# Four layers over eight items: the next item's opening at the end of the search's stream, setup in two parts, a new weaving table

## What is computed

```python
x = L0_attn_x                                   # 8 x 512 x 128
xn = _layernorm(x, axis=-1)
s = _L0_attn_ref(xn, Wq, Wk, Wv, Wbeta, Wg, Wout, ln_g, ln_b)   # 16 heads of 8: recurrence over tokens
g = _silu(_L0_ffn_ref(xn, ...))                 # a small network, three cycles
x = x + s * g
...
s = _L1_attn_ref(xn, ...)                       # two time-mixing layers
g = _silu(_L1_ffn_ref(xn, ...))                 # two layers of attention in windows of 64, and an ffn
...
s = _L2_attn_ref(xn, ...)                       # state space: 256 channels x 16 states
g = _silu(_L2_ffn_ref(xn, ...))                 # 4 experts, 2 per token
...
s = _L3_attn_ref(xn, ...)                       # 16 heads of 8: softmax kept to each row's 25 largest, and a linear part
g = _silu(_L3_ffn_ref(xn, ...))
```

```python
q = _l2norm((x @ Wq).reshape(b, s, nh, d))
k = _l2norm((x @ Wk).reshape(b, s, nh, d))
beta = jax.nn.sigmoid(x @ Wbeta)
out = out * jax.nn.silu(x @ Wg)
```

## Time and profile before

| | us |
|---|---|
| three runs: median (lowest to highest) | 5226.68 (5222.0 to 5237.3) |
| the profiled execution's own time | 5220.98 |
| its span, first to last instruction | 5219.2 |
| PE, DVE busy | 3965.6, 3970.4 |
| ACT, POOL busy | 2966.9, 2533.0 |
| PE's mean granted clock | 0.822 |

### The profile page before, as it was taken

One profiled execution on the slowest core, in us unless ns is written; L12 is line 12 of the kernel. 1 busy time (PEld: TensorE's weight loads), 2 busy tenths in 40 slices (PEclk: granted clock), 3 DMA queues, 4 the chain that ended last, 5 costly groups with the idle time before them and its releaser, 6 DMA issues. The chain is left out here.

```text
span 5219.2 us, 58396 instructions
## 1 busy us (share of the span) xinstructions
PE 3965.6 (76%) x16712; PEld 1848.2 (35%) x16712; DVE 3970.4 (76%) x7862; ACT 2966.9 (57%) x5742; POOL 2533.0 (49%) x2332
## 2 busy tenths in 40 slices
PE   5777788868878678777788677886887777877676
PEld 2332244423443234432344224442344323443233
DVE  3335678967889678886888868896788967888698
ACT  3443556645666456655666466664566645665443
POOL 1214255453555445562555625545455545556365
PEclk9876889968998789977899688996899878997555
DMA  1000000000000000000000000000000000000000
GB/s 81 1 25 0 5 1 1 25 3 3 1 25 1 3 3 1 25 1 3 3 1 25 1 5 1 8 18 3 3 1 25 1 3 3 1 25 1 2 1 3
DMA packets 7995, 44.07 MB, mean 8 GB/s; under 512 B 848, under 2 KB 848, under 8 KB 7248
## 3 DMA queue, kind: packets, MB, share of 16 engines
q1 hardware_dynamic: 7632, 39.89, 2.0%
HBM read 37.52 MB, written 2.36 MB: 8 GB/s over the span
## 5 line engine op out<-in xcount | busy, mean ns | idle before, releaser
L2054 DVE MAX8 m<-top 128x8 f32<-128x512 f32 x2048 | 1290.7, 679 | 6.4 <-ACT top L1988 5.9
L2117 POOL TENSOR_SCALAR top<-top,m 128x512 f32<-128x512 f32 x512 | 809.9, 1582 | 836.6 <-DVE m L2054 670.2
L2058 DVE MATCH_REPLACE8 top<-m,top 128x512 f32<-128x512 f32 x1536 | 1026.3, 675 | 0.2
L290 PE MATMUL bank<-arena,consts 128*128 128x512 f32 (+1 forms) x912 | 627.7, 782 | 90.7 <-POOL arena L1662 45.4
L2123 POOL TENSOR_TENSOR top<-top 128x512 f32<-128x512 f32 x512 | 654.6, 1278 | 37.5 <-ACT top L1996 20.2
L290 PE MATMUL bank<-arena,weights 128*128 128x512 f32 (+5 forms) x992 | 553.9, 678 | 65.8 <-DVE arena L1242 29.0
L1927 PE MATMUL bank<-consts,top 128*128 128x128 f32 x2048 | 389.5, 322 | 210.6 <-POOL top L2123 128.7
L290 PE MATMUL bank<-arena 128*64 128x128 f32 (+3 forms) x3200 | 464.3, 366 | 54.4 <-ACT arena L1105 53.8
L2003 ACT ACTIVATE top<-bank 128x512 f32<-128x512 f32 x512 | 305.5, 597 | 296.4 <-PE bank L1927 294.8
L1927 PEld LDWEIGHTS bank<-consts,top 128*128 128x128 f32 x2048 | 283.2, 165 | 489.8 <-POOL top L2123 274.8
L290 PE MATMUL bank<-top,vt 128*9 128x128 f32 x4096 | 340.7, 321 | 151.8 <-ACT top L2003 128.2
(11 more groups left out here) (297 smaller groups left out, 6436.9 us busy)
## 6 DMA issues: line engine op xcount, KB each, us to landing
arena<-experts_dram SPq DMA_DIRECT2D x32, 768.0 KB, 6.6
weights<-weights_dram SPq DMA_DIRECT2D x1, 6982.0 KB, 19.2
hold<-x_dram SPq DMA_DIRECT2D x9, 256.0 KB, 2.8
out_dram<-x_out SPq DMA_DIRECT2D x9, 256.0 KB, 3.5
consts<-consts_dram SPq DMA_DIRECT2D x1, 1759.5 KB, 23.6
rot<-consts_dram SPq DMA_DIRECT2D x1, 1024.0 KB, 25.6
```

The costliest lines, as they stand in the source:

```text
L290: return nc.tensor.matmul(o, lhsT, rhs, start=start, stop=stop)
L2054: nc.vector.max(m8[:, slot(p, e), k], src).then_inc(SB["top"], 1)
L2058: nc.vector.match_replace(wk_[e], m8[:, slot(p, e), k], sc[slot(p, e)] if k == 0 else wk_[e], -3e38).then_inc(SB["rest"], 1)
L2117: nc.gpsimd.tensor_scalar(pp[e], sc[slot(p, e)], m8[:, slot(p, e), TOPK // 8, 0:1], None, ALU.is_ge).then_inc(SB["kept"], 1)
```

## The change

1. The opening goes to the end of stream b, eight steps behind the search, for the item of the *next* block. It uses the search's banks (`O`) and tiles of `top`, waits for the `x0` load and for the search's last readers, and DVE's `xn0` waits for layer 2's `du`. Layer 0 starts with V. A new block between setup and `run(0, ...)` computes item 0's opening; item 1's stands at the end of item 0's block, where stream b idles for as many steps as a search has. The loop's last pass computes an opening that nobody reads.
2. Layer 2's gate tile moves out of `hold` (`spare[3]` is the next item's `sg`) and its last product goes to `L.xr`.
3. Setup waits for three loads: the first 1,938 columns of the weights, `x0` and the constants. The rest of the weights and `rot` are waited for in layer 0 of item 0, from its 13th step (`also`), where the moved arithmetic stands (`late_pe`, `late_act`, `late_dve`).
4. `SEARCH` has new digits. Stream a is now 192 steps without the opening (200 before), b 258 (250).

```diff
-SEARCH = ("0100001101010110313101111102014430103203524241042002012030121030211001100413012310002320321101061200"
+SEARCH = ("0211001223120111101111012062132022120226313101020020023111203i02730013205201221133211120011101101110"
...
-                    sp.dma_start(w_sb[:], w_in).then_inc(S["loaded"], 16)
+                    sp.dma_start(w_sb[:, 0:cut], w_in[:, 0:cut]).then_inc(S["loaded"], 16)
                     sp.dma_start(x0, x_in[0]).then_inc(S["loaded"], 16)
                     sp.dma_start(c_sb[:], c_in[:, 0:once]).then_inc(S["loaded"], 16)
-                    sp.dma_start(rot[:].rearrange("p n t -> p (n t)"), c_in[:, once:]).then_inc(S["loaded"], 16)
+                    sp.dma_start(w_sb[:, cut:], w_in[:, cut:]).then_inc(SL["rest"], 16)
+                    sp.dma_start(rot[:].rearrange("p n t -> p (n t)"), c_in[:, once:]).then_inc(SL["rest"], 16)
...
-                    v.wait_ge(S.sem["loaded"], 64)
+                    v.wait_ge(S.sem["loaded"], 48)
...
+        O = [X[1], Y, P, X[0]]
...
-                self.sq, self.rs, self.ksq, self.qsq, self.rk, self.rq, self.beta = (carve() for _ in range(7))
+                self.sq, self.rs, self.ksq, self.qsq, self.rk, self.rq, self.beta = *sc, *ex, wk_[0]
...
-            def pe(self, pe):
+            def pe(self, pe, item, search):
                 S = self.S
-                mm(A[0], C("centre"), x0).then_inc(S["op_xc"], 1)
+                if item:
+                    pe.wait_ge(SD.sem["x0"], 16)
+                if search:
+                    pe.wait_ge(*SB("sc", 2 * NP))
+                    pe.wait_ge(*SB("of", 1))
+                    pe.wait_ge(*SB("took", NT))
+                mm(O[0], C("centre"), x0).then_inc(S["op_xc"], 1)
...
-                mm(self.last, W("l0_Wg"), xn0).then_inc(S["op_g"], 1)
+                if search:
+                    pe.wait_ge(*SB("m", 1))
+                mm(O[3], W("l0_Wg"), xn0).then_inc(S["op_g"], 1)
...
+                if item:
+                    v.wait_ge(*S2("du", 1))
                 v.wait_ge(*S("op_rs", 1))
-                tt(xn0, A[0], self.rs, ALU.mult).then_inc(S["op_xn"], 1)
+                tt(xn0, O[0], self.rs, ALU.mult).then_inc(S["op_xn"], 1)
...
-            yield from L.op.pe(pe)
             cp = L.cp.pe(pe)
-            pe.wait_ge(*S("op_kn", 1))
-            pe.wait_ge(*S("op_qn", 1))
             mm(A[1], W("l0_Wv"), xn0).then_inc(S["v"], 1)
...
+        def b_pe(pe, item, search):
+            if search:
+                cp = Layer3.cp.pe(pe)
+                yield from l3_pe(pe, cp)
+            else:
+                yield from idle("search " * SEARCH_STEPS)
+            if item:
+                yield from (opening if search else lead).pe(pe, item, search)
...
+        def also(steps, more):
+
+            for n, kind in enumerate(steps):
+                if n >= 12:
+                    next(more, None)
+                yield kind
+            for _ in more:
+                pass
...
-            yield from l0_pe(pe)
+            yield from also(l0_pe(pe), late_pe(pe)) if first else l0_pe(pe)
...
+        with nc.Block(no_gpsimd_drain=True) as block:
+            @block.tensor
+            def _(pe):
+                weave(lead.pe(pe, False, False), None)
...
+        lead_marks.settle()
+        clear(top_marks.sems.values())
         run(0, True, False)
```

More of the change, by code:

```diff
@@ L715, in build @@
             POOL=f"nmx {2 * NP},kept {2 * NP},pp {2 * NP}")
+        opening = Opening(top_marks.layer(**OPENING))
+        lead_marks = Marks(nc, ctx, "b")
+        lead_marks.sems = top_marks.sems
+        lead = Opening(lead_marks.layer(**OPENING))
         class Layer0:
@@ L830, in l0_pool @@
             S, L = S0, Layer0
-            yield from idle("hop hop hop hop hop hop hop hop")
             cp = L.cp.pool(g)
-            g.wait_ge(*S("op_sg", 1))
             nc.gpsimd.tensor_scalar(L.sgb, sg, W("l0_ln_b"), None, ALU.mult).then_inc(S["shifted"], 1)
@@ L1350, in __init__ @@
                 L.nm = L.carve(NT)
-                L.sq, L.rs, L.left, L.gate = spare[0:4]
+                L.sq, L.rs, L.left = spare[0:3]
+                L.gate = L.carve()
                 L.xg = [spare[4], L.xr]
@@ new lines, in b_act, with b_dve @@
+        def b_act(a, item, search):
+            if search:
+                cp = Layer3.cp.act(a)
+                yield from l3_act(a, cp)
+            else:
+                yield from idle("search " * SEARCH_STEPS)
+            if item:
+                yield from (opening if search else lead).act(a)
+        def b_dve(v, item, search):
+            if search:
+                cp = Layer3.cp.dve(v)
+                yield from l3_dve(v, cp)
+            else:
+                yield from idle("search " * SEARCH_STEPS)
+            if item:
+                yield from (opening if search else lead).dve(v, item)
@@ new lines, in b_pool, with late_pe @@
+        def b_pool(g, item, search):
+            if search:
+                cp = Layer3.cp.pool(g)
+                yield from l3_pool(g, cp)
+            else:
+                yield from idle("search " * SEARCH_STEPS)
+            if item:
+                yield from idle("hop " * 8)
+        def late_pe(pe):
+            S = SL
+            pe.wait_ge(S.sem["rest"], 32)
+            for n, (name, part) in enumerate((name, part) for name in ("gamma", "beta") for part in range(2)):
+                r = nc.tensor.transpose(X[0][:, 128 * n:128 * n + 128], W(f"l3_{name}", lo=128 * part, n=128), C("ident"))
+            r.then_inc(S["by_channel"], 1)
+            for i in range(DEPTH):
+                for n, name in enumerate(("Wk", "Wv", "Wr")):
+                    mm(X[1][:, DEPTH * n + i:DEPTH * n + i + 1], W(f"l1_{name}{i}"), W(f"l1_ln_b{i}"))
+                for n, (o, w) in enumerate(HCH):
+                    at = 8 + 6 * i + 2 * n
+                    mm(X[1][0:w, at:at + 1], W(f"l1_w1_{i}", lo=o, n=w), W(f"l1_lb{i}"))
+                    r = mm(X[1][0:w, at + 1:at + 2], W(f"l1_w1_{i}", lo=HID + o, n=w), W(f"l1_lb{i}"))
+            r.then_inc(S["shifts"], 1)
+            yield
@@ L2177, in a_dve @@
         def a_dve(v, first):
-            yield from l0_dve(v, first)
+            yield from also(l0_dve(v, first), late_dve(v)) if first else l0_dve(v, first)
             yield from l1_dve(v)
```

183 lines of the change are left out of this document (89 added, 94 removed).

## The result

| | before | after |
|---|---|---|
| median (lowest to highest), us | 5224.93 (5222.0 to 5237.3) | 5134.86 (5130.29 to 5150.64) |
| the profiled execution's own time | 5220.98 | 5130.29 |
| its span | 5219.2 | 5128.5 |
| PE's mean granted clock | 0.822 | 0.822 |

A forecast was written before the change was run, and what follows sets the result against it. Bound by neither one engine nor one chain: two streams whose in-order queues hold each other up, with a bare block start. Setup -25.7 + 8, item 0's tail +10, loop -39.2: total -46.9, 5174 us; range 5105 to 5240.

The forecast's parts named there:

- Part 1, the start: Start of each block: the opening leaves it and V comes first, gaining 16.6 us, net 13.6 a block.
- The norm of the search: Block start: the search's norm now stands between layer 0's matmuls; cost 3 us a block, between 0 and 6.7.
- Part 2, the end: State loop's end: the opening placed there costs 8 us in a middle block and 10 in item 0.
- the ring: Item 0's state loop: 4.07 us round a state, PE in it at the low clock, so added matmuls are paid.
- The rival's 5114: State loop's end and block start: opening hides better, tail 3.3 and norm 0 in place of 8 and 3; chance 0.18.
- The full stall: State loop: the opening's chain overlaps nothing, 18.0 and two table loads, 20.6 us a block; 5273, slower; chance 0.10.
- Part 3, setup: Setup in two parts: loads land 17.3 us earlier, arithmetic shrinks by 11.4, new boundary costs 3; net -25.7.
- the new boundary: Behind the first opening, with 12 clears per engine: taken as 3 us, between 0 and 8.
- The late work: Item 0's layer 0: setup arithmetic moved there, 40 matmuls of 8.2 us and a sigmoid; costs 8, between 0 and 10.8.
- Part 4, the table: Search steps redistributed across the block: counted as 0, with -5 and +10 us a block as ends.
- the rival's size: Layer 1's first attention: the item stands 24.5 us, thinned places return little over half; +10 a block, 5244; chance 0.12.
- the burst: Layer 1's first attention: 18 search steps in one gap, 24.5 us in which the item stands.

The follow-up runs named there:

- experiment 1: Changed kernel with the old table up to the state loop and the new table inside it: 5128.14 us, ratio 0.9800 against the kernel before.
- experiment 2: Kernel before with the new table alone, behind eight zeros for the opening's steps: 5302.05 us, ratio 1.0143.
- experiments 4 and 5: Changed kernel, loop's opening replaced by cheap stand-ins: 5146.27 us; the same with eight unread matmuls put back at its places on PE: 5136.68 us.
- experiment 6: Kernel before with the matmul that spreads B issued twice in each of the 16 states: 5230.19 us, ratio 1.0004.
- Experiment 3: Changed kernel with all eight steps of the opening behind the layer's last instruction, at the block's very end: 5289.34 us, ratio 1.0115 against the kernel before.
- experiments 9 and 10: Changed kernel with a bigger burst, 34 search steps in one gap: 5241.31 us; with the old table ahead of the states and 22 steps in one gap: 5292.66.
- experiment 7: Changed kernel with setup waiting for all five loads again: 5146.49 us (two runs), ratio 0.9839 against the kernel before.

## Why the prediction was right, and where its sizes were off

The direction, the range (5105 to 5240) and most mechanisms held. The forecast's gain of 47 stands against 90.7 by the two spans: 30 of the missing 44 us are in the loop, 11 in item 0, 2 in the last search. That the total fell well inside the range is partly luck. The forecast added up the moved opening and the new table as if one did not change the other's price, and counted the table at nothing. Measured one behind the other in the profiled blocks, with the table first, the table costs 10.3 a block and the opening then gains 20.5; with the opening first it gains 6.8 and the table another 3.4. Either way the sum is 10.2, where the forecast had 5.6.

- **Part 1, the start.** 16.6 forecast, 17.1 measured. The norm of the search was counted at 3, and no cost of it shows (in experiment 1 the start fell by 17.8, V's share was 16.8): the lower of the two ends that the prediction kept.
- **Part 2, the end: the term that was mis-sized most.** "At the low clock PE is in the ring, so a matmul put there is paid" was worked out from item 0's ring, and gave 8 a block and 10 in item 0. Measured is 5.2 beside the old table (experiment 1), and -2.3 beside the new one (217.3 to 215.0, experiment 2 against the change). In item 0, from the experts' loads to the store, it is 188.5 in place of 189.3. Two things in the ring's sum were wrong. It left the clock where it was: the added matmuls came with a granted 0.73 in place of 0.50 (experiments 4 and 5; the kernel before, with the old table, had 0.61 to 0.66 there), and in item 0 with 0.83 between 480 and 500, where the stretch that lies as far ahead of the store before, 499 to 519, had 0.50:

```profile
480.00:500.00 20.00, 14.11 (x27) 5.06 (x28) 13.61 (x14) 12.37 (x19) 16.14 (x10) 0.83 0.00 0
```

  And it read the ring as closed: experiment 6 put up to 10 us of PE work in it for 0.4 to 1.9 a block, and for 2.8 in item 0. The prediction had this as a rival ("high clock in the tail, because it adds PE work, and a free norm") and set against it that item 0 was at 0.50; but that was the clock without the work that the change puts in. The rival's 5114 overshoots by 16 against the profiled execution: 13.3 a block in place of 9.9, with the table at nothing.
- **The full stall** is refuted for this place. Experiment 3 gives the size that the rival had without its table loads, 18.0 a block, for an opening laid behind the states. The price of a table load is 1.28 us as before. In item 0's opening after the change, ACT:

```profile
25.57 1.28 ACT L311 ACT_TABLE_LOAD   x1
26.86 0.69 ACT L606 ACTIVATE top<-bank,consts 128x512 f32<-128x512 f32 x1
```

  The next ACTIVATE starts 0.01 us behind the load. The Trainium skill (ScalarE: Activation LUTs, What ACT_TABLE_LOAD costs) states a drain of 1.38 us besides; this trace again shows none, and the price would have moved the sum away from the result.
- **Part 3, setup.** -25.7 forecast and -25.8 measured at V (landing 10.43 against 10.5 forecast; the new boundary, from `u`'s end at 30.66 to V at 32.83, 2.2 against 3). The late work was counted at 8. From V to the experts' load item 0 took 289.65 in place of 282.01: 7.6 more, 2.0 of it up to the `x0` load and 5.6 behind it. In the other runs with the same late work it was 287.6 to 290.9, of which 64 to 71 us up to the `x0` load. So the term's size was right, but not its reason: the 40 matmuls took 0.60 + 3.79 = 4.4 us in place of the 8.2 of the earlier trace rows, in a stretch at the high clock (1.00 from 68 to 74). Where the rest of the 7.6 lies was not taken apart.
- **Part 4, the table.** 0 forecast, with -5 and +10. As a part of the change it is about neutral (experiment 1). But it isn't so alone: in the kernel before it costs 10.3 a block (experiment 2), the rival's size for another reason. The forecast weighed only the burst. What the table takes from the block's start is given back nearly one for one (9.2 for 9.4), what it takes from the end is not (12.2 for 19.1), unless the opening stands there: in the change the end is 14.5 shorter than before for 16.6. A cost of the burst itself does not show (the middle grew by 31.6 with 31.2 to 31.5 of DVE work); experiments 9 and 10 show what makes a burst cost, steps taken from the gaps behind it.
- **The sum by what was measured**: first store -19.0 in place of -7.7 (-25.8 at V, +7.6 to the experts' load, -0.8 from there; forecast -25.7, +8 and +10); loop -69.4 in place of -39.2; last search -2.3 in place of 0.

One block of the seven is 8 us longer than the others (615.5, the middle 304.8). Within its second attention 0.50 was granted, with PE busy 16.9 of 20 us:

```profile
3879.70:3899.70 20.00, 16.89 (x82) 9.30 (x82) 10.34 (x28) 10.29 (x36) 8.50 (x11) 0.50 0.00 0
```

In the middle block the stretch as far behind the store (3272 to 3292) had 0.74. Two of seven blocks had a middle of 304 to 305 in experiment 2, none in experiment 7. What triggers one was not tried and stays open.

## What to carry to other kernels

A dependent chain of small operations that stands bare at a boundary is worth its length when it is laid between the steps of another loop, and costs that length again when it is laid bare elsewhere (18.0 us behind the states; between them 5.2 beside the old table and less than nothing beside the new one). Two edits that use the same room have no price of their own each: run each alone and both together before the terms are added up. Sum the busy time of the fullest engine by stage, before and after: where a stage's length and that work change alike (31.6 and 31.5), the work was only moved, and the gain is in the stage whose idle time fell. When filler work is concentrated, look at the gaps that it is taken from: a full engine cost nothing here, but the serial stretch behind it must keep its cover.

## What the runs showed of the hardware

Matmuls added to a stretch in which PE was granted half clock cost less than their durations at that clock: eight of 128x512 made the end 1.8 us shorter (217.3 to 215.5), with the grant 28 to 13 us ahead of the store going from 0.50 in all seven blocks to 0.70 to 0.73, and the output matmul behind them taking 1.99 us in place of 3.78. Sixteen of up to 0.63 us, spread over all states of the kernel before, cost 0.4 to 1.9 a block, and 2.8 in item 0. A busy PE was not always granted more: in the run with the bigger burst it stood at 0.50 for 50 us on end (3222 to 3272), busy 5.9 to 8.5 us of each ten.
